# Decoder layer on one core: cross scores from fp32 operands, and the same scores from bf16 high and low parts

## The reference, cut to what matters

```
qx = ln(fp8_linear(ln_out, wqx)).reshape(b, s, g, hpg, d)      # 112 rows, 16 heads
kx, vx = split(einsum('bsi,oi->bso', cond, w_kv_x))            # 375 rows, 8 groups
kx = ln(kx)
scores = einsum('bsghd,btgd->bghst', qx, kx) / sqrt(128)       # 112 x 375 each
xout = einsum('bghst,btgd->bsghd', softmax(scores), vx)
```

## Time and profile before

| | |
|---|---|
| median of 3 runs | 1170.13 us (1168.93 to 1170.41) |
| the profiled execution | 1168.96 us |
| its span | 1167.2 us |
| busy in the span | PE 1125.7, DVE 843.8, ACT 809.7, POOL 617.4 us |
| PE instructions | 6269 |
| granted TensorE clock | 0.99 of full speed over the span |

### The profile page before, as it was taken

How to read it: one execution, slowest core, us unless ns; L and a number is a source line. 1 busy time by engine, 2 the same in 40 slices (tenths; PEclk the granted TensorE clock), 3 DMA queues, 4 the chain that set the end, 5 groups by cost and what they waited for, 6 DMA issues and landing times.

```text
span 1167.2 us, 20352 instructions
## 1 busy us (share of the span) xinstructions
PE 1125.7 (96%) x6269; PEld 765.5 (66%) x6330; DVE 843.8 (72%) x2761; ACT 809.7 (69%) x2348; POOL 617.4 (53%) x761
## 2 busy tenths in 40 slices
PE   4899999878999999999999999999999999999998
PEld 2577776656767777667667666677766766554564
DVE  4768996899877886768787786757876786675242
ACT  5667756978887988667777776667877678675130
POOL 1645895685464555526464464526544472366172
PEclk9999999999999999999999999999999999999999
DMA  9436342132220113123332223222331210000000
GB/s 284 161 116 203 115 134 75 56 108 73 74 65 27 55 37 109 36 90 108 118 94 88 76 77 99 72 81 74 98 130 51 90 37 10 1 1 1 37 2 28
DMA packets 36204, 92.97 MB, mean 80 GB/s; under 512 B 3568, under 2 KB 13936, under 8 KB 36096
## 3 DMA queue, kind: packets, MB, share of 16 engines
q1 hardware_dynamic: 35824, 91.30, 24.2%
q10 hardware_dynamic: 272, 0.36, 0.1%
HBM read 74.07 MB, written 17.58 MB: 79 GB/s over the span
## 4 chain that ended last, share of the span: by engine, by line
PE 79%; DVE 8%; ACT 4%; DMA 3%; issue 2%; POOL 2%; SPq 1%; ACTq 0%; DVEq 0%
PE ps L1148 16%; PE ps L1141 11%; PE ps L1247 8%; PE ps L1218 8%; PE ps L1202 8%; PE ps L1174 6%; PE ps L1259 4%; PE ps L1183 4%; PE ps L1160 4%; PE ps L1056 3%; PE ps L1171 2%; PE ps L1068 2%; DMA big<-in_w_v 2%; DMA big<-in_w_s 2%; DVE big L1763 1%
## 5 line engine op out<-in xcount | busy, mean ns | idle before, releaser
L1148 PE MATMUL ps<-big 128*125 128x512 bf16 x960 | 220.4, 379 | 0.3 <-ACT big L1502 0.3
L1502 ACT ACTIVATE big<-ps,big 112x128 f32<-112x128 f32 (+1 forms) x512 | 192.6, 460 | 15.1 <-POOL big L2059 13.7
L1141 PE MATMUL ps<-big 128*112 128x512 bf16 x768 | 184.7, 384 | 8.8 <-ACT big L1549 6.7
L2057 POOL TENSOR_TENSOR big<-big 112x4 f32<-112x4 f32 (+1 forms) x128 | 48.0, 375 | 235.9 <-ACT big L1313 235.3
L1148 PEld LDWEIGHTS ps<-big 128*125 128x125 bf16 x960 | 127.5, 136 | 64.6 <-ACT big L1502 0.5
L1634 DVE BATCH_NORM_STATS2 big<-ps 112x6 f32<-112x128 f32 (+1 forms) x512 | 113.3, 283 | 40.3 <-PE ps L1148 27.5
L1141 PEld LDWEIGHTS ps<-big 128*112 128x112 bf16 x768 | 97.1, 131 | 62.1 <-ACT big L1549 7.1
L1561 ACT ACTIVATE big<-ps 125x336 f32<-125x336 f32 x96 | 43.4, 452 | 111.7 <-PE ps L1183 111.4
L1202 PE MATMUL ps<-big 125*128 125x224 f32 (+1 forms) x512 | 118.1, 352 | 1.3
L2069 POOL TENSOR_TENSOR big<-big 128x448 f32<-128x448 bf16 x64 | 70.6, 1103 | 86.4 <-DVE big L1926 86.3
L1202 PEld LDWEIGHTS ps<-big 125*128 125x128 f32 (+1 forms) x512 | 96.6, 190 | 14.3
(11 more groups left out here) (128 smaller groups left out, 2397.7 us busy)
## 6 DMA issues: line engine op xcount, KB each, us to landing
big<-cs SPq DMA_DIRECT2D x16, 750.0 KB, 4.5
big<-in_w_s SPq DMA_DIRECT2D x16, 512.0 KB, 4.6
big<-in_w_p SPq DMA_DIRECT2D x16, 512.0 KB, 5.2
big<-in_w_x SPq DMA_DIRECT2D x16, 512.0 KB, 4.0
big<-in_w_g SPq DMA_DIRECT2D x16, 512.0 KB, 5.5
big<-in_ctx_t SPq DMA_DIRECT2D x12, 500.0 KB, 7.1
cs<-big SPq DMA_DIRECT2D x24, 250.0 KB, 3.6
big<-in_w_d SPq DMA_DIRECT2D x8, 512.0 KB, 5.1
```

Of the source, the lines that this page charges most:

```text
L1141: t = e.matmul(bk[0:T, :], xq[:, k, :], wt[:, s, k, col:col + 512], start=k == s == 0, stop=k == 3 and s == 1)
L1148: t = e.matmul(bk[0:CK, :], ctxT[:, c, s, k, :], wt[:, u, k, col:col + 512], start=k == s == u == 0, stop=k == 3 and s == 1)
L1502: t = e.activation(z[0:rows, 128 * j:128 * j + 128], ps(("p_mm", n))[0:rows, 128 * j:128 * j + 128], ACT.Identity, bias=v["q"][:, j:j + 1] ...
```

## The change

The cross part's q and k are split as the other operands are. ACT's `p_t` writes the fp32 result into one of two scratch buffers of 512 words (`qk_words`, given out by a ring of two, `split_slot`). A new DVE step `p_hi`, last in DVE's tick, copies it to bf16; a new POOL step `p_lo`, last in POOL's tick, subtracts this high part from the fp32 value and writes the low part. `t_s0` waits for `p_lo` of the batch's last k or q, and makes three bf16 matmuls in place of the fp32 one. The waits for a free `q_sb` or `kX` move from ACT's `p_t` to DVE's `p_hi`. The two scratch buffers lie where stage buffer 3 was: it is taken out of use at the first projection of the cross part (tick 64), and three are left. All orders are otherwise the same.

```
             else:
-                t = e.matmul(bk[0:T, 0:SC], q_sb[i][:, 2 * g + one, :], kX[i][:, g, :], start=True, stop=True)
+                for s, u in ((0, 0), (0, 1), (1, 0)):
+                    t = e.matmul(bk[0:T, 0:SC], qX[i][:, s, 2 * g + one, :], kX[i][:, u, g, 0:SC],
+                                 start=s == u == 0, stop=s == 1)
...
-            w.wait_ge(*qk_sb[last_no(h, b, "qk")])
+            w.wait_ge(*(qk_sb if S else qk_lo)[last_no(h, b, "qk")])
...
+            if not S:
+                dst = qk_whole(n)
+                for free in split_slot.after["p_t", n]:
+                    w.wait_ge(*free)
...
+        def p_hi(n):
+            if not in_parts(n):
+                return
...
+            w.wait_ge(*qk_sb[n])
+            e.tensor_copy(qk_part(n, 0), qk_whole(n)).then_inc(qk_hi.sem, 1)
...
+        def p_lo(n):
+            if in_parts(n):
+                w.wait_ge(*qk_hi[n])
+                e.tensor_tensor(qk_part(n, 1), qk_whole(n), qk_part(n, 0), ALU.subtract).then_inc(qk_lo.sem, 1)
...
+        crossing = crossing or (s == "p_mm" and k == proj_no("X0", 0, "q", 0))
+        if crossing and 3 in [i for i, _ in stage.idle]:
+            ends = stage.retire(3)
+            for i in range(2):
+                split_slot.reset(i, *ends)
```

More of the change, by code:

```diff
@@ L100, in give, with retire @@
         self.idle.append((self.of[user], ends))
+    def retire(self, slot):
+        ends = [e for i, e in self.idle if i == slot][0]
+        self.idle = [x for x in self.idle if x[0] != slot]
+        return ends
     def reset(self, slot, *ends):
@@ L286 @@
         ("b", 3, "b_mask"), ("a", 5, "t_mag"), ("b", 4, "b_3"), ("b", 1, "b_1"), ("b", 3, "b_2"), ("a", 1, "t_s1"),
[1 row of a table added]
     ],
     "POOL": [
-        ("p", 1, "p_rstd"), ("a", 5, "t_s4"), ("b", 3, "b_2"), ("b", 1, "b_1"),
+        ("p", 1, "p_rstd"), ("a", 5, "t_s4"), ("b", 3, "b_2"), ("b", 1, "b_1"), ("p", 3, "p_lo"),
     ],
@@ L416, in _program @@
     aXQV = whole.take(5376)
-    whole.take(20)
+    whole.take(28)
     aXQX = whole.take(1792)
@@ L577, in is_v, with in_parts, qk_part, qk_whole @@
         return PROJ[n][2] == "v"
+    def in_parts(n):
+        return PROJ[n][0][0] == "X" and not is_v(n)
+    def qk_part(n, part):
+        _, b, what, c = PROJ[n]
+        if what == "q":
+            return qX[b % 2][:, part, 4 * c:4 * c + 4, :]
+        return kX[b % 2][:, part, :, CK * c:CK * c + CK]
+    def qk_whole(n):
+        rows = T if PROJ[n][2] == "q" else CK
+        return qk_words[split_slot.of["p_t", n]][:, 0:4 * rows].rearrange("p (g t) -> p g t", g=4)
     def proj_before(h, b):
@@ L860, in place @@
                 bank.give((s, k), qk_sb[k])
+                if in_parts(k):
+                    split_slot.take((s, k))
+        elif s == "p_lo":
+            if in_parts(k):
+                split_slot.give(("p_t", k), qk_lo[k])
         elif s == "p_mm":
@@ L1525, in p_t @@
                 wt, bs = vc[:, o:o + 1], vc[:, o + 1:o + 2]
[L1526 to L1536, removed]
+                dst = kS[b % 2]
+                if nb < 2:
+                    w.wait_ge(*a_score[27 + 4 * nb])
+                elif S:
+                    hb = divmod(nb - 2, NB)
+                    w.wait_ge(*score[att_no(HALVES[hb[0]], hb[1])])
+            if not S:
+                dst = qk_whole(n)
+                for free in split_slot.after["p_t", n]:
+                    w.wait_ge(*free)
             e.activation(dst, ps(("p_t", n))[:, 0:4 * rows].rearrange("p (g t) -> p g t", g=4), ACT.Identity,
@@ L1830, in p_stats @@
                 ln_halves(("p_stats", n), ps(("p_mm", n)), p_rows(n), 4, 128)
+        def p_hi(n):
+            if not in_parts(n):
+                return
+            h, b, what, _ = PROJ[n]
+            if what == "q":
+                hb = divmod(NB * HALVES.index(h) + b - 2, NB)
+                w.wait_ge(*score[att_no(HALVES[hb[0]], hb[1])])
+            else:
+                for free in x_free(h, b, score):
+                    w.wait_ge(*free)
+            w.wait_ge(*qk_sb[n])
+            e.tensor_copy(qk_part(n, 0), qk_whole(n)).then_inc(qk_hi.sem, 1)
         def p_aggr(n):
@@ L2102, in d_0 @@
             e.tensor_tensor(sm[:, 1:2], sm[:, 0:1], cf[:, C_HALF:C_HALF + 1], ALU.pow).then_inc(f_rstd.sem, 1)
[L2104 removed]
+        mine = dict(p_lo=p_lo, a_rot=a_rot, l_q=l_q, b_1=b_1, b_2=b_2, p_rstd=p_rstd, t_s4=t_s4, g_1=g_1, d_0=d_0)
         for s, k in steps["POOL"]:
```

22 lines of the change are left out of this document (14 added, 8 removed), and 4 rows, old and new, of tables (ORDER, ORDER_X).

## The result

The change made the kernel slower: 1185.13 us (median of 5 runs, 1181.47 to 1187.8) against 1170.16 us (median of 5, 1168.93 to 1171.04), a ratio of 1.0129 with a 95% interval of 1.0113 to 1.0145. The forecast was 1161 us, faster. The profiled execution took 1187.8 us, its span 1185.9.

What follows compares the result with a forecast made beforehand. PE, with 2.7 us idle in the 560 us cross part, was taken as the bound. Cheaper score products save 19.5 us, head stalls return 10.5, so 9.0 off the profiled 1168.96, plus 1.17 to the median: 1161 us, range 1151 to 1168.

Steps and rivals of the forecast that it cites:

- The 32 and 92 us: Cross part: time added by 80 copies on DVE and 80 subtractions on POOL, taken as hidden on average.
- the head path: Batch heads: the first score now waits for DVE's copy, then POOL's subtraction; five batches give back 10.45 us.
- The collision: A DVE instruction beside a POOL one can pay 0.9 us; considered at four batch heads, only in a range.
- The clock: PE in the cross part: granted clock left at 1.00, since PE stays as busy.
- The head stalls: PE waits at batch heads: 4.7 us at 2, 1.4 at 4, 1.5 at 6, 2.1 at 10, 0.75 at 1.
- The slower rival: Every batch head: copies meet POOL instructions and queue, scores wait; typically 1178 us, chance 0.12.
- the products' 0.48 us a head: Scores on PE: three bf16 matmuls take 0.478 us for 0.63, saving 19.5 us over 128 heads.
- weight loads hidden: Scores on PE: 128 more loads of 0.131 us, covered by matmuls of 0.159 us, cost nothing.
- the stage buffer at nothing: Weight loads with three buffers: ACT waits up to 1.1 us three times, covered by its idle time, cost 0.
- the third rival: Stage buffers: late weight loads on ACT also cost 6.3 us, giving 1165 to 1168 us; chance 0.14.
- the calm batches' 1.2 us: Calm batches of the cross part: each 8 × 0.152 = 1.2 us shorter, of 34.5 us.
- POOL's durations: The new subtraction on POOL: 1.1 us for q and 1.2 us for k.

Runs made afterwards that it cites:

- e12: e2 with three stage buffers and 80 POOL subtractions on scratch data that nobody waits for: 1166.95 us.
- e7: e12 with 80 DVE copies on scratch data as well, nobody waiting for either operation: 1181.36 us.
- e3: The changed kernel, but scores wait for the copy alone and multiply the high parts three times; POOL's subtraction still runs: 1177.25 us.
- e2: The kernel before, four stage buffers, ACT writing q and k straight to bf16, high parts multiplied three times, no low parts: 1154.11 us.
- e6: The changed kernel without POOL's subtraction; scores wait for the copy and multiply the high parts three times: 1160.64 us.
- e18: The changed kernel, whole, with the F and X1 units of weights moved to other ticks, fewer F units meeting splits: 1169.74 us.
- e9: The changed kernel with the subtraction on DVE, right behind the copy, and nothing new on POOL: 1204.53 us.
- e19: e18's moved units in the version where ACT makes the high and DVE the low part (1172.92 us with old placing): 1175.56 us.
- e1: The kernel before with only the fourth stage buffer taken out of use at the first cross projection: 1169.84 us.

## Why the prediction was wrong

**The sign fell with one step: costing the copies and subtractions at nothing "on average".** The 32 and 92 us were "hidden on average", and the only loss allowed for them was the head path, 10.5 us. e12 and e7 measure what they cost when nobody waits for them: 27.2 us; with their real waits, but no head waiting for a low part, it is 23.1 us (e3 against e2). The head path, priced at 10.5 us, measured 7.9. Had the load cost nothing, about 15.8 − 7.9 = 7.9 us would have been left as a gain, close to the 9.0 forecast. The prediction had the rows for it: DVE at 81% and POOL at 82% in the burst, DVE's 1.75 us wait for POOL and 24.5 us in all. It used these rows for the head of batch 2 and the average for all the rest. In the burst the two engines are no two pools of free time but one ring, POOL L2105 to DVE L1866, L1921, L1859 to POOL L2103. That the load is dear is shown by e3, e6, e7 and e12; that it is dear because it lengthens this ring is read from one burst. e18 supports it for 15.4 us, and e9 and e19 don't follow from it alone.

**The collision was the second miss.** I priced it at 0.9 us, four times, in a range only. The price was right (L1921 1.25 us against 0.41), the count was not: 28 of the 48 `b_3` are long where 5 were. DVE's `b_3` went from 515 ns in e2 to 911 as a mean over 48, L1850 and L1841 in e7 by 168 and 198 ns, and the new copy, priced at 0.38 us for q and 0.41 for k, took 0.73 and 0.50 us on average (shortest of all 0.378, longest 1.366). The Trainium skill, page "SBUF — State Buffer", section "Who interferes with whom", names casts, `tensor_scalar` and DVE instructions with two SBUF inputs among those that can contend with GpSimd, and says that the port pair they share is held for the whole instruction by whoever issues first, while the other waits. The trace agrees: `b_3` at 684.54 and L1921 at 685.83 end 0.3 and 0.2 us after POOL's L2095 and L2110. What I had left out is that a further POOL instruction stretches DVE's old instructions, and not only its new ones.

**The clock.** "PE stays as busy, so I leave it there" rested on the step above and fell with it. Around the wait of 3.70 us:

```profile
684.00:691.00 7.00, 6.95 (x37) 4.45 (x37) 4.71 (x7) 3.09 (x7) 6.30 (x6) 1.00 0.06 20
691.00:698.00 7.00, 3.30 (x13) 2.16 (x12) 6.93 (x22) 2.37 (x7) 5.33 (x6) 0.68 0.78 258
698.00:705.00 7.00, 6.95 (x31) 4.75 (x31) 4.53 (x24) 5.25 (x16) 3.57 (x7) 0.83 0.06 23
```

The clock is 1.00 before it, 0.68 over the 7 us with the wait, and 0.83 in the next 7 us, where PE is busy again: part of them went at the lower of the two levels, 1.2 GHz. The first matmuls after it take 1.16 us for three, 0.64 at 657.51. Over the span the mean falls from 0.994 to 0.984, which is worth at most 12.0 us more than before.

**The head stalls.** Named were batches 2, 4, 6, 10 and 1, with 10.45 us. Found were 4.28, 1.29, 3.70 and 2.74 us at 2, 4, 6 and 10, nothing at 1, and 0.56 to 1.25 us at batches 8, 11, 12 and 13: 15.6 us. Four of the five places and the size of batch 2 (4.7 forecast) were right; the waits are worth 7.9 us of the end (after against e3). The slower rival had "the score wait at every head through collisions": it had the sign and the collision, and its time, 1178, but not the place, since with nobody waiting for a split (e7) the kernel is still at 1181.

**Right were:** the products' 0.48 us a head (the term as a whole was 3.7 us too large: 15.8 measured against 19.5, e2); weight loads hidden (PE busy for 557.6 of 560 us in e2); the stage buffer at nothing (e1, and after the change ACT waits for a transfer of weights twice from 480 to 1040, for 1.9 and 0.2 us), so the third rival falls; the calm batches' 1.2 us; POOL's durations (1.05 us for q, 1.18 for k; 1.1 and 1.2 forecast).

**The balance by experiments:** 1169.9, less 15.8 for the products, plus 12.8 for the subtractions' and 14.4 for the copies' load, makes 1181.4 (e7). The remaining 3.7 us to 1185.1 go by that balance to the new waits (e3 against the change gives them 7.9: the parts don't simply add). By the steps that keep the real waits it is 6.5 for the copies, 16.6 for the subtractions and 7.9 for the new waits, 31.0 in all. Of these, 15.4 go with the placing of the units (e18). Not told apart is what makes up the other 15.6: the 20 `b_2` that still share a tick with a split, stretched instructions (L1850 stays at 1003 ns), single late heads, and the clock (10.5 us by the ledger's measure in e18, 8.1 in e2).

## What to carry to other kernels

Where two engines hand work to and fro and a saturated third one depends on them, cost an added instruction in the busiest stretch, on the round of work that they pass between them, not against idle time averaged over the kernel; and add, for each POOL instruction, the DVE instructions that will stand beside it. When PE is saturated, a saving on it is a debt of the other engines: each must deliver that much sooner, and a wait of 3 to 4 us can cost PE more than itself: here the granted clock was 0.83 in the 7 us after the one of 3.70 us. Before giving up such a change, move it in time: here the same instructions cost 15.4 us less with the units of weights on other ticks. Then run the kernel before with the moved units too, which wasn't done here.

## What the runs showed of the hardware that I had not expected

- DVE instructions without any new dependency lengthened on average from 838 to 1006 ns, 515 to 918, and 353 to 551 (e2 against e7), nearly all of it by the subtractions alone (e12: 1007, 939, 508), while L1859, bf16 from two bf16 inputs, stayed at 0.41 us in every kernel. There POOL can be the one that pays: L1859 took 0.41 us at 680.54 after the change, and POOL's L2141 of 192 columns, begun at 680.37, took 1.29 us, against a mean of 0.55 for that form before.
- Two loads that cost 12.8 us (e12) and 6.5 us (e6) alone cost 23.1 together (e3).
- Runs of one and the same kernel differed by 6.3 us with a mean clock of 0.984 and 0.990; e2's runs, with PE saturated, lie within 1151.91 and 1154.51 at 0.991 to 0.993.
